# Rebuilding the per-batch half of a soft mixture-of-experts and recurrence kernel: statistics through HBM, slot weights spread by DMA, and every second chunk product in three rounded passes

## What is computed

```python
xn = layernorm(x)                                  # 16 sequences x 512 tokens, width 128
Q = xn @ Wq + bq                                   # attention with Q = K = V
s = softmax(Q @ Q.T / sqrt(128)) @ Q
logits = (xn @ phi_w.T + phi_b).reshape(.., 64, 32)   # 64 experts x 32 slots
D, C = softmax over the slots, softmax over the experts
X_tilde = einsum(D, xn); layernorm over width, tanh
Y_tilde = X_tilde @ expert_w + expert_b            # per expert
g = silu(einsum(C, Y_tilde))                       # C x Y: 2048 slots contracted
x = x + s * g
xn = layernorm(x)
s = rmsnorm(scan(h = a * h + gated)) @ W_out       # gates from xn
g = silu(sigmoid(xr @ W_r) * (relu(xk @ W_k)**2 @ W_v))   # xr, xk mix xn with the token before
x = x + s * g
```

## Time and profile before

| | us |
|---|---|
| median of 3 runs (lowest to highest) | 1346.94 (1345.48 to 1347.56) |
| the profiled execution | 1348.3 |
| its span, first to last instruction | 1346.2 |
| PE, DVE, ACT, POOL busy | 1252.0, 1051.1, 740.2, 814.2 |

### The profile page before, as it was taken

How to read it: one execution, slowest core, us unless ns; L and a number is a source line. 1 busy time by engine, 2 the same in 40 slices (tenths; PEclk the granted TensorE clock), 3 DMA queues, 4 the chain that set the end, 5 groups by cost and what they waited for, 6 DMA issues and landing times.

```text
span 1346.2 us, 17623 instructions
## 1 busy us (share of the span) xinstructions
PE 1252.0 (93%) x4866; PEld 740.7 (55%) x4866; DVE 1051.1 (78%) x1533; ACT 740.2 (55%) x1459; POOL 814.2 (60%) x768
## 2 busy tenths in 40 slices
PE   6699999999999999998699999999999999999984
PEld 2465555555555555553465555665555565555641
DVE  6899999999999999996455777666776667776653
ACT  2655556556665555653434555555655555655554
POOL 3588989999898898996244454343453344453320
PEclk9899999999999999999799999999999999999997
DMA  6433333333333333333643333333333333333310
GB/s 199 120 139 124 141 128 137 140 125 140 134 131 141 124 140 131 134 141 141 196 133 118 102 125 117 111 125 110 118 123 105 125 118 110 117 110 125 125 32 16
DMA packets 123217, 167.35 MB, mean 124 GB/s; under 512 B 7153, under 2 KB 99313, under 8 KB 122993
## 3 DMA queue, kind: packets, MB, share of 16 engines
q1 hardware_dynamic: 122688, 164.65, 35.5%
q10 hardware_dynamic: 434, 1.59, 0.4%
HBM read 90.71 MB, written 75.50 MB: 123 GB/s over the span
## 4 chain that ended last, share of the span: by engine, by line
PE 37%; POOL 5%; DVE 4%; issue 4%; ACT 0%; POOLq 0%; DVEq 0%
PE yac L797 12%; PE ct L785 6%; POOL b_e L1331 5%; PE at L854 4%; PE at L844 2%; DVE nmx L1180 2%; PE lp L894 1%; PE lp L906 1%; PE lp L900 1%; DVE b_ti L1259 1%; PE lp L139 1%; PE lp L869 1%; PE at L830 1%; PE at L833 1%; PE at L832 1%
## 5 line engine op out<-in xcount | busy, mean ns | idle before, releaser
L562 POOL TENSOR_TENSOR dd<-ed,rz 128x512 f32<-128x512 f32 x256 | 263.4, 1050 | 58.9 <-DVE rz L551 58.9
L463 PE MATMUL acc<-dd,xns 128*128 128x512 f32 x512 | 260.9, 592 | 1.3 <-POOL dd L562 1.3
L797 PE MATMUL yac<-cf,expert_out 128*128 128x512 f32 x512 | 261.7, 594 | 0.0
L1167 DVE TENSOR_TENSOR cf<-ct,slot_weight 128x512 f32<-128x512 f32 x256 | 175.3, 685 | 87.1 <-PE ct L785 84.1
L498 ACT ACTIVATE ed<-lg 128x512 f32<-128x512 f32 x256 | 138.9, 595 | 84.7 <-PE lg L448 84.7
L538 DVE TENSOR_REDUCE mr<-lg 128x32 fp32r<-128x1024 f32 x128 | 154.6, 1208 | 26.0 <-PE lg L434 26.0
L785 PEld LDWEIGHTS ct<-identity,exp_slots_loaded 128*128 128x128 f32 x1024 | 127.7, 142 | 80.1 <-issue 67.3
L570 POOL TENSOR_TENSOR slot_weight<-exp_slots_loaded 128x512 f32<-128x512 f32 x128 | 164.5, 1286 | 0.0
L432 PE MATMUL lg<-phi_transposed,xn_transposed 128*128 128x512 f32 x256 | 158.4, 619 | 2.2 <-PEq L359 1.8
L504 ACT ACTIVATE exp_slots_loaded<-lg 128x512 f32<-128x512 f32 x256 | 139.0, 595 | 30.3 <-PE lg L454 30.2
L546 DVE TENSOR_REDUCE zd<-ed 128x32 f32<-128x1024 f32 x128 | 154.8, 1209 | 1.0 <-ACT ed L498 1.0
(11 more groups left out here) (187 smaller groups left out, 2242.0 us busy)
## 6 DMA issues: line engine op xcount, KB each, us to landing
exp_slots<-exp_slots_loaded SPq DMA_DIRECT2D x128, 512.0 KB, 2.7
exp_slots_loaded<-exp_slots SPq DMA_DIRECT2D x128, 512.0 KB, 3.4
xns<-xn_rows SPq DMA_DIRECT2D x128, 64.0 KB, 1.7
expert_w<-in_expert_w SPq DMA_DIRECT2D x8, 512.0 KB, 5.3
b_xraw<-in_xT SPq DMA_DIRECT2D x16, 256.0 KB, 3.7
out_t<-b_ti SPq DMA_DIRECT2D x16, 256.0 KB, 4.1
xn_rows<-slot_max SPq DMA_DIRECT2D x2, 1024.0 KB, 5.1
xn_rows<-slot_sum SPq DMA_DIRECT2D x2, 1024.0 KB, 5.3
```

What stands on the lines that cost most here:

```text
L463: e.matmul(acc[k][:, :], xns[w % RX][:, :], dd[w % RX][:, bank(k)], start=tile == 0, stop=tile == NT - 1, skip_group_check=True).then_inc( ...
L562: e.tensor_tensor(dd[v % RX][:, bank(k)].rearrange("q (n p) -> q n p", p=NP), ed[c][:, bank(k)].rearrange("q (n p) -> q n p", p=NP), rz[c] ...
L797: e.matmul(yac[:, :], YF[:, c, :], cf[c % RC][:, :], start=c == 0, stop=c == CH - 1).then_inc(c_y)
L1167: e.tensor_tensor(cf[c % RC][:, :], ct[c % 2][:, :], WT[i % 2][c // (CH // HALVES)][:, :], ALU.mult).then_inc(c_w)
```

## The change

What it does, by place:

- In block 1 the statistics SM and SS are also stored to a DRAM tensor (`slot_statistics`), in four DMAs during the block and two after it. From block 1b on each join loads its batch's part (`join_load`, two DMAs issued by SP) into small tiles. SM and SS no longer live into block 2, which frees SBUF there.
- The joined slot weights are no longer made four times over. `join_weights` writes 128x256, `join_turned` takes two transposes (now at step 5, into `lp[1]`), `join_copied` one copy (ACT step 6), `join_stored` writes it to DRAM and `join_spread` reads it back with eight DMAs of 32 partitions each. `state_mean` now also waits for that copy, since both use `lp[1]`.
- In block 1b a high part (YHI, rounded to fp32r) and a low part (YLO, the rest) of the eight odd chunks of `expert_out` are made.
- In block 2 `combine` of an odd chunk is three fp32r passes: high x high, low x high, high x low. The high part of `cf` is an ACT copy (`high`), the low part a POOL subtraction (`low`). `weigh` becomes three passes too, with `turn_low` and `value_low` on DVE.
- `weighted_rows` and the rounding of the query and of the normalised input move to ACT; `silu_y` and `y_copy` read `yac` in PSUM directly, and the first product into `yac` waits for `silu_y`; `mean` multiplies with identity minus mean, so `centre` and `keep` go; `mix_previous` becomes one `difference` on POOL; the square of the feed-forward moves from ACT to POOL; several pieces stand at other steps.

The core of the diff:

```diff
+        def join_load(e, b):
             if b:
                 e.wait_ge(s_wp, WP * b)
-            e.tensor_tensor(MJ[:, :, :], joined(SM, b)[:, 0], joined(SM, b)[:, 1], ALU.max).then_inc(s_wv)
+            for k, dst in ((0, MS), (1, ZS)):
+                e.dma_start(dst[:, :, :, :], STATS[:, k, :, b * TPB:(b + 1) * TPB, :]).then_inc(s_st, 16)
+
...
+        def join_stored(e, b):
+            e.wait_ge(s_wc, b + 1)
+            if b >= 2:
+                e.wait_ge(s_wl, 16 * WL * (b - 1))
+            e.dma_start(WD[b % 2].rearrange("h r k -> r h k"), WS[:, :, :]).then_inc(s_wd, 16)
+
+        def join_spread(e, b):
+            e.wait_ge(s_wd, 16 * (b + 1))
+            for j in range(EPC):
+                for h in range(HALVES):
+                    e.dma_start(WT[b % 2][j * NP:(j + 1) * NP, h, :].rearrange("p (t k) -> p t k", t=TPB),
+                                WD[b % 2][h].rearrange("(t p) k -> p t k", p=NP)).then_inc(s_wl, 16)

...
+                e.wait_ge(s_stat, 64)
+                join_load(e, 0)
+                for k, src in ((0, SM), (1, SS)):
+                    e.dma_start(STATS[:, k, 1, EARLY:NT, :], src[:, 1, EARLY:NT, :]).then_inc(s_stat, 16)
                 for k in range(RE):
-                    e.wait_ge(s_est[k], 16 * (UNITS // RE))
+                    e.wait_ge(s_exp[k], STORED)
                 for g in range(RL):
                     load_exps(e, g)
+                join_stored(e, 0)
+                join_spread(e, 0)
+                join_load(e, 1)
                 for g in range(RW, GROUPS):
                     e.wait_ge(s_yf, (g - RW + 1) * CPG)
                     load_experts(g)
+                e.wait_ge(s_stat, 96)
...
+                        if k == 3 and i + 1 < NB:
+                            join_stored(e, i + 1)
+                        if k == 4 and i + 1 < NB:
+                            if i:
+                                e.wait_ge(c_w, i * CH)
+                            join_spread(e, i + 1)
                         if k == 5:
                             store(i - 2)
+                            if i + 2 < NB:
+                                join_load(e, i + 2)
...
-                    e.matmul(yac[:, :], YF[:, c, :], cf[c % RC][:, :], start=c == 0, stop=c == CH - 1).then_inc(c_y)
+                        e.wait_ge(S["u_y"], i)
+                    if c % 2 == 0:
+                        e.wait_ge(c_w, g + 1)
+                        e.matmul(yac[:, :], YF[:, c, :], cf[g % RF][:, :], start=c == 0, stop=False).then_inc(c_y)
+                        return
+                    k = g // 2
+                    e.wait_ge(c_h, k + 1)
+                    e.matmul(yac[:, :], YHI[:, c // 2, :], chi[k % RO][:, :], start=False, stop=False)
+                    e.matmul(yac[:, :], YLO[:, c // 2, :], chi[k % RO][:, :], start=False, stop=False)
+                    e.wait_ge(c_l, k + 1)
+                    e.matmul(yac[:, :], YHI[:, c // 2, :], clo[k % RO][:, :], start=False, stop=c == CH - 1).then_inc(c_y)

...
+                        e.wait_ge(s_wc, min(i + 4, NB))
...
                             weigh(i, 0)
-                        if c == 11:
-                            weights_turned(i + 1, 0)
-                            weights_turned(i + 1, 1)
+                        if c == 5:
+                            weights_turned(i + 1)
...
+                def high(i, c):
+                    if within(i) and c % 2:
+                        g = i * CH + c
+                        k = g // 2
+                        e.wait_ge(c_w, g + 1)
+                        if k >= RO:
+                            e.wait_ge(c_y, g - 2 * RO + 1)
+                        e.activation(chi[k % RO][:, :], cf[g % RF][:, :], ACT.Copy).then_inc(c_h)
...
+                        if c == 4:
...
                             attended(i - 1)
                         if c == 2:
                             value_high(i)
-                        if c == 4:
-                            input_scale(i - 2)
+                            if i + 1 < NB:
+                                join_factors(e, i + 1)
+                        if c == 5:
+                            weighted_rows(i, 0)
+                        if c == 6:
+                            weighted_rows(i, 1)
+                            if i + 1 < NB:
+                                join_copied(e, i + 1, lp[1])
                         if c == 7:
+                            weighted_rows(i, 2)
+                            weighted_rows(i, 3)
                             squares(i - 1)
                         if c == 8:
                             state_norm(i - 2)
                         if c == 9:
                             turn_high(i, 0)
                             deviation(i - 1)
+                            if within(i - 1):
+                                e.preload_act_table_set("exp_and_others")
+                        if c == 10:
...
+                            ffn_k_positive(i - 1)
                         if c == 14:
                             ffn_r_tanh(i - 1)
                         if c == 15:
                             turn_high(i, 3)
+                        high(i, c)
                         if c == 0:
                             query(i)
                         if c == 2:
...
-                            if i + 1 < NB:
-                                join_factors(e, i + 1)
                         if 3 <= c < 7:
                             probabilities(i, c - 3)
                         if c == 5:
                             state_squares(i - 2)
-                        if c == 9 and within(i - 1):
-                            e.preload_act_table_set("exp_and_others")
-                        if c == 11:
-                            if i + 1 < NB:
-                                for h in range(HALVES):
-                                    join_copied(e, i + 1, h, lp[h])
...
+                        if c == 0:
+                            e.wait_ge(s_wl, 16 * WL * (i + 1))
+                        if g >= RF and c % 2:
+                            e.wait_ge(c_l, (g - RF) // 2 + 1)
+                        elif g >= RF:
+                            e.wait_ge(c_y, g - RF + 1)
...
+                def value_low(i):
+                    if within(i):
+                        e.wait_ge(S["v_h"], i + 1)
+                        e.tensor_tensor(R["vl"][:, :], at[1][:, :], hi_f32(R["vh"][:, :]), ALU.subtract).then_inc(S["v_l"])
+
+                def turn_low(i, k):
+                    if within(i):
+                        e.wait_ge(A["kh"], i * TPB + k + 1)
+                        e.tensor_tensor(ptl[k % 2][:, :], at[1][:, :], hi_f32(pth[k % 2][:, :]), ALU.subtract).then_inc(A["kl"])
...
+                        if c == 2:
+                            value_low(i)
                         if c == 3:
                             silu_y(i - 1)
+                        if c in (9, 11, 13, 15):
+                            turn_low(i, (c - 9) // 2)
                         if c == 4:
                             weights(i, 0)
+                            if i + 1 < NB:
+                                join_inverse(e, i + 1)
...
-                        if c == 7 and i + 1 < NB:
-                            join_inverse(e, i + 1)
...
+                def low(i, c):
+                    if within(i) and c % 2:
+                        g = i * CH + c
+                        k = g // 2
+                        e.wait_ge(c_h, k + 1)
+                        e.tensor_tensor(clo[k % RO][:, :], cf[g % RF][:, :], hi_f32(chi[k % RO][:, :]), ALU.subtract).then_inc(c_l)
...
```

369 lines of the change are left out of this document (188 added, 181 removed), and 4 rows, old and new, of the table S.

## The result

The changed kernel takes 1410.18 us at the median of four runs (1409.22 to 1414.6), the kernel before 1347.25 beside it (1345.48 to 1348.34): a ratio of 1.0475, 95% interval 1.045 to 1.05. The forecast was 1405. The profiled execution took 1414.6, with a span of 1412.8; the other three took 1409.2 to 1410.2, and where its 4 us more are likely to lie is told at the end.

The account below looks back on a forecast made before the run. PE was taken to bound block 2; its work falls to 36.5 us a round, but waits make rounds 44.3. Block 2 +46.5 and block 1b +12 give 58.5 on the median 1346.94: 1405 us, range 1352 to 1430.

Parts of the forecast that it names:

- rival D: Block 2: PE's count rules and its waits stay at 1.8 us a round, 38.3 in all; total 1320 us; chance 9%.
- The seven waits: PE's waits in a full block 2 round: six new, the old one for exp tiles gone; sum 7.9 us.
- waits 4 and 6: Step 6, `state_mean` waits for the square and `join_copied`, +2.5 us; step 12, `ffn_k` waits for `decay_tanh`, +1.3.
- wait 2: Block 2, step 3: `combine(0)` waits for `silu_y`, since `yac` is read in place; +1.3 us a round.
- 1 and 5: Block 2: step 0, `project` waits for `attended`, +0.6 us; steps 10 to 12, waits at `weigh(1)` and `decay_gate`, +1.1.
- wait 3: Block 2, step 5: `join_turned` waits for POOL's `join_weights`; +1.1 us a round.
- The walk: One full block 2 round followed with PE's new list: 44.3 us, 3.5 more than 40.81.
- Block 2 in sum: +46.5 us: 13 full rounds x 3.5, round 0 -2, round 1 +1, round 15 +3, tail -0.5.
- Block 1b: +12 us: statistics land late, `join_max` about 648.5, last expert loads issued at 664.6, block 2 starts about 675.
- The rule weighed: fp32 products: by the notes' four passes, three save 0.215 us, total some 10 lower; the forecast took the rows' 0.16.
- At nothing: Four extra stores in block 1, eight spreading DMAs in block 2 and the block 1 overlays cost no time.
- Rival B: Block 2: waits partly hidden, only 3, 4 and one other stay, +0.7 us a round; total 1368 us; chance 16%.

Follow-up runs that it names:

- k1: Changed kernel with ACT's copy of the joined weights and square of the state ahead of chunk 5's high copy and score tile 2's exp; 1385.44 us.
- k7: k6 with the high copy of chunk 11 alone placed behind `decay_tanh` on ACT; 1369.37 us.
- k8: k7 with `silu_y` ahead of DVE's first row maximum, k4's edit, and two of block 1b's last four expert loads ahead of the spreading; 1351.91 us.
- k5: Changed kernel with the odd chunks as single fp32 products again, without their high copies on ACT and subtractions on POOL; 1372.17 us.
- k2: Changed kernel with PE's two transposes of the joined weights ahead of step 6 instead of step 5; 1414.99 us.
- k6: Changed kernel with the edits of k1 and k2 together; 1383.97 us.
- k12: Changed kernel with the edits of k5, k1 and k2, k8's `silu_y` and block 1b edits, and six expert-weight buffers; 1322.31 us.
- k4: Changed kernel with batch 0's two statistics loads issued ahead of the expert and bias loads in block 1b; 1405.98 us.
- k3: Changed kernel with every high copy of an odd chunk moved to the end of the next step on ACT; 1468.27 us.

## Why the prediction was right

**The bound.** PE bounded the kernel before, and the count of its work after was right: 36.5 forecast, 36.3 measured as the rest of the round. The forecast did not stop at that count (rival D's step, 1320); that the gain becomes idle time was the point.

**The seven waits.** All six new ones are there, by the releasers named, each within 0.2 us, in sum 7.9. The old one for the exp tiles is gone. k1 and k7 show for waits 4 and 6 that the lists' order makes them, and k8 shows it for wait 2 (1.16 us of idle before, 0.4 in k8). That 1 and 5 go with the copies and subtractions, k5 shows, though not by order alone. For wait 3 the price by itself depends on what is next: nothing in k2 and k6, 0.56 a round in k12.

**The walk's form mattered.** It gives waits in a chain, each measured from where PE is after the one before. That is why its sum was right, though the waits cannot be removed one by one at their full length. My expectations for k5 and k6 took them singly, and both missed.

**Block 2 in sum.** +52.8 in the profiled execution, forecast +46.5. Start to first scan: -0.4 (forecast -2 and +1). Twelve rounds from scan to scan: 534.5 against 489.8, 44.7 more, of which 12 x 3.45 = 41.4 are waits as forecast and 3.4 are two rounds of 45.9, in which PE's clock halved. The rest, a last full round and the end: +8.5 against 6.0. Here too the clock took part: PE's clock is at half from about 1343 to 1346.5, and the two scans around it are 37.41 apart, where k2, without such a stretch there, has 35.73. The last two scans are 25.46 apart, where k2 and k4 have 24.06 and 23.99; that is likely the clock as well. Without these 3.1 the rest is +5.4. So the end was sized about right, and what the sum lacked is a term for the clock.

**Block 1b.** +13.8 against 12. The front was right to 0.2. Behind it two errors cancelled in part, which is luck: the store landed after 1.8 us and not 2.7, and the ten issues behind it took 5.5 and not 3.5 (660.22 to 665.72). So the last expert loads were issued 1.1 later than forecast; PE could begin on the first of them 4.1 later, where I had 3.7, and the remainder was 7.6 and not 7.2. The last copy of X_tilde waits for POOL as I had said, and delays nothing: it ends at 632.8, DVE's last slot sum at 633.6. That block 1b began 0.5 later is within the scatter (in k2, with the same code, 1.9 earlier than in the kernel before). k4 confirms the cause of the front's delay, and shows that the end hangs on a second cause.

**The total.** These parts are from the two profiled executions and add up to 52.8 + 13.8 = 66.6. The medians are 62.9 apart, 4.4 more than the forecast 58.5; the profiled execution of the changed kernel was its slowest.

**The rule weighed.** A step of transposes and three passes takes 1.13 to 1.15 us (1023.66 to 1024.79 in the round above), and one of transposes and an fp32 product 0.43 + 0.86 = 1.29: 0.15 a product, as the prediction took from the rows (0.16). The Trainium skill (FP8 and Floating Point Precision, TensorE Precision Notes) gives four passes for fp32, and 0.86 is four times 0.215. But the three fp32r passes of a step are not 0.215 each: their starts, with that of the next instruction, are 0.32, 0.24 and 0.22 apart. So three instead of four do not save 0.215.

**At nothing.** The eight spreading DMAs in block 2 and the stores in block 1: PE never waits there for a DMA in this trace. That holds.

**Rival B** had a point that the forecast lacked: a wait can hide in the next. It hid edits here, though, and not the change.

## What to carry to other kernels

When the bound engine gets less work, walk one full round of every in-order list with its new, earlier arrival times: what it gains it may only wait. A short operation put into a waiting engine's list costs what stands behind it, not its own time: here the copies of 0.63 us, with the subtractions behind them, cost PE more than the products that they made cheaper saved. Before a wait is removed, read how long the next one's releaser is already done; that slack is what can be gained, and the same edit was worth nothing, nothing and 0.56 us a round in three settings. Place such a copy behind what the bound engine wants next, but look at who is queued behind its consumer too: moving all of them a step lost 58 us, moving one gained 15.

## What I had not expected of the hardware

**PE's clock after a wait.** With waits of at most 1.2 us in the steady part (k1) the granted clock stayed at 1.00. With one of 2.08 in each round (the changed kernel) it stayed there in most rounds and fell to half, 1.2 GHz, in two (in k4, with the same wait, in one). PE had been idle from 1252.34:

```profile
1252.00:1254.00 2.00, 0.34 (x1) 1.00 0.00 0
1254.00:1256.00 2.00, 1.59 (x2) 0.59 0.00 0
1256.00:1258.00 2.00, 2.00 (x7) 0.55 0.00 0
```

Each cost 1.68 us (rounds of 45.94 and 45.92 among 44.26). k2's wait is 3.2 long: five of its twelve full rounds are of 45.7 to 47.0 among 44.24, 10.2 us in sum against 3.4. A round without it is as long as in the changed kernel, so this is the likely source of the 4.8 us more in its median. It is not shown: the profiled execution of k2 was its fastest, 1413.6, and 1.0 us below the changed kernel's, since its block 2 started 2.5 us sooner and it gained in the first and last rounds. k3, with a wait of 3.0, has a halved clock in each of the twelve rounds, so the length of one wait does not decide it alone. What the traces show is that k2, which has the changed kernel's waits of 1.0 and 2.1 in one, lost more to the clock than the changed kernel did: merging waits can lose though their sum stays. Which rounds are hit differs even between the changed kernel and k4, whose block 2 is the same. The clock is also the likely reason why the profiled execution of the changed kernel (mean clock 0.967) took 4 us more than the other three (0.973 to 0.978); that was not tried by itself.

**A wait costs more than its bracket.** Each wait cost 0.15 to 0.3 us more than the idle time that the profile names (1.16 named, 1.42 lost; 0.27 named, 0.55 lost). Of this, 0.16 is a matter of counting: a product's record ends 0.16 behind the point where the next can start (1.02 long, 0.86 apart; 0.40 and 0.23 for a pass). Only the other 0 to 0.12 is a slower first instruction.

**A small store behind loads.** The store of 128 KB landed 6.4 us after its issue where four loads of exponentials had been issued just before (k4), and 1.8 after it where none had been for 10 us (the changed kernel). The forecast had 2.7.
